# Ranking token scores: comparisons summed on VectorE, and comparisons summed by TensorE products with a column of ones

## The chip, the cores and the metric

The kernel runs on one core of one Trainium2 chip. The metric is the time on the device in microseconds (us). Three runs of the kernel before took 2085.96, 2092.15 and 2094.51 us; the median is 2092.15 us.

## The reference, cut to what matters

The model embeds 4 sequences of 1024 tokens (192 numbers each) and sends them through two layers. The change touches one step of the first layer's feed-forward block: a router scores every token, and the 154 tokens with the lowest scores (15% of 1024) get attention.

```
scores = jax.nn.sigmoid(jnp.einsum('bld,d->bl', normed, Wr) + br)
k = max(1, int(round(ROUTE_FRAC * l)))
_, idx = jax.lax.top_k(-scores, k)
attn_mask = jnp.zeros((b, l), bool).at[jnp.arange(b)[:, None], idx].set(True)
...
merged = jnp.where(attn_mask[..., None], attn_out, mix_out)
```

The order among the selected tokens has no meaning, but every one of them needs a slot of its own. The kernel gives each token its rank, the number of tokens of its sequence that come before it: those with a lower score, and of those with the same score the ones at an earlier position.

## The kernel before, in words

The four sequences are worked on as two pairs (`p` = 0, 1), one after the other. The two sequences of a pair live in two slots, `a` (x = 0) and `z` (x = 1), and nearly every step of the program is written as "for both slots". Tokens lie on partitions in T = 8 blocks of P = 128; L is 1024. There is no scheduler: each engine has its program written out by hand, runs it strictly in that order, and waits on semaphores. `link` lets an engine wait for the end of its own last instruction.

Around the change the order is this, on each engine:

- TensorE: `scores_row` for slot a, then `scores_row` for slot z. Each turns the scores from partitions into a row that is copied on all 128 partitions (8 transposes, L591), and then sums the tokens weighted by score: 24 products with a column of scores, N = 1 (L596). Then `pick` for slot a and for slot z (L603): 16 products that gather the selected tokens. Then `queries0` for both slots (L536, L551).
- ScalarE: copies the row of scores to SBUF, `srow` (L1191), for a and z; later it copies out what `pick` gathered (L1195).
- VectorE: `rank_tokens` for slot a, `pool_tokens` for slot a, then the same two for slot z. `rank_tokens` holds the change.

`rank_tokens` before: for each block t of 128 tokens, whose scores `sc[:, t]` lie one on a partition, VectorE compares the whole row `srow` with the partition's score and sums the ones of each partition in the same instruction (`accum_out`). The tokens from block t on are compared with "lower" (L1366), those of earlier blocks with "lower or equal" (L1368), and a 128x128 piece settles equal scores inside the block with the mask `earlier` (L1369). The three counts are added (L1371, L1372). From the ranks come `notsel` (L1374) and the selection matrix `PSEL` (L1376), whose semaphore `picks` releases `pick` on TensorE.

In the trace an instruction of VectorE with a sum shows as two records, the work and a short DVE_READ_ACCUMULATOR. One product of f32 operands shows as two matmuls and two weight loads (LDWEIGHTS), and a bf16 product as one of each; such a load with its matmul is called a pass below. The names in the trace: `R` holds `srow`, `Er` is a large work area (junk of the comparisons and `PSEL`), `PV` and `MT` are the PSUM banks `o.O` of slots a and z, `ST` and `S` are other PSUM banks.

Of the kernel before, what the change touches and what calls it, by code (L numbers as in the profile page):

```python
# [12 lines left out]
P = 128  # L13
# [4 lines left out]
L = 1024  # L18
# [66 lines left out]
def build(nc, A, out):  # L85
    ctx = ExitStack()
    with ctx:
        def sb(name, shape, dt=F32):
            return ctx.enter_context(nc.sbuf_tensor(name, shape, dt))
# [7 lines left out]

        ident = sb("ident", [P, P])
        identb = sb("identb", [P, P], BF16)
        earlier = sb("earlier", [P, P])  # L100
        ones = sb("ones", [P, P])
        neghalf = sb("neghalf", [P, T])
        slot = sb("slot", [P, 2, QP])
# [51 lines left out]
        junkg = acc_out[:, :, :].rearrange("p a n -> p (a n)")[:, 0:F]  # L155
        acc_mem = sb("acc_mem", [P, HALF])
        junk2 = sb("junk2", [P, P])
        vsum = junk2[:, 0:4 * VC].rearrange("p (t d) -> p t d", t=4)
        nmp = sb("nmp", [P, T, 2])
        nm = sb("nm", [P, T, 2])  # L160
# [8 lines left out]
        for x in range(2):  # L169
            o = Slot()  # L170
            slots.append(o)
            o.x = x
            nx = str(x)
            o.s = {n: sem("s_" + n + nx) for n in OWN}
            o.X = sb("X" + nx, [P, T, D])
            o.U = sb("U" + nx, [P, T, D])
            o.HS = sb("HS" + nx, [P, T, D])
            o.V = sb("V" + nx, [P, T, H, VC])
            o.XT = sb("XT" + nx, [CH + 1, 2, L])
            R = sb("R" + nx, [P, 4 * (L + 2)])  # L180
            o.R = R
            o.XC = R[0:CH, 0:2 * (L + 2)].rearrange("p (c n) -> p c n", c=2)
            o.CUM = o.XC[:, :, 2:L + 2]
            o.Y1 = R[0:CH, 2052:2052 + L]
            o.Z = R[0:CH, 3076:3076 + L]
            o.spl = R[0:CH, 0:3 * L].bitcast(BF16).rearrange("p (a c n) -> p a c n", a=3, c=2)
            o.srow = R[:, 3 * L:4 * L]
            o.PT = R[:, 0:2 * L].rearrange("p (q n) -> p q n", q=2)
            o.hid = R[:, 0:FC * HALF].rearrange("p (f n) -> p f n", f=FC)
            o.kc = R[0:CH, 0:3 * HALF].bitcast(BF16).rearrange("p (a n) -> p a n", a=3)  # L190
            o.qc = R[0:CH, 3 * HALF:6 * HALF].bitcast(BF16).rearrange("p (a n) -> p a n", a=3)
            o.BT = R[0:CH, 0:2 * L].rearrange("p (c n) -> p c n", c=2)
            o.HG = R[:, 0:HT * F].rearrange("p (t f) -> p t f", t=HT)
            o.PSEL = Er[:, x * W0:(x + 1) * W0].rearrange("p (t n) -> p t n", t=T)
            low, mid = Er[:, x * 1792:x * 1792 + 768], Er[:, x * 1792 + 768:x * 1792 + 1792]
            o.XQ = low.bitcast(BF16).rearrange("p (t d) -> p t d", t=T)
            o.XQT = mid[0:CH, :].bitcast(BF16).rearrange("p (c n) -> p c n", c=2)
            o.e2 = mid[:, 0:768].rearrange("p (i t d) -> p i t d", i=2, t=2)
            o.HQ = low.bitcast(BF16)
            o.HQT = Er[:, 3584 + x * 768:3584 + (x + 1) * 768].bitcast(BF16).rearrange("p (t f) -> p t f", t=2)  # L200
            o.QS0 = sb("QS0" + nx, [KP + 4, H, 2 * QP], BF16)
            o.NTS = sb("NTS" + nx, [CH + 1, 2, 2 * QP])
            o.CXT = o.NTS
            small = sb("small" + nx, [CH, 6 * QP])
            o.spl0 = small[:, :].bitcast(BF16).rearrange("p (a c n) -> p a c n", a=3, c=2)
            o.CX = small[0:QP, 0:2 * D].rearrange("p (q d) -> p q d", q=2)
            o.ATS = sb("ATS" + nx, [QP, 2, D])
            flat = o.X[0:QP, 0:3, :].rearrange("p t d -> p (t d)")
            o.sum0 = flat[:, 0:24 * VC].rearrange("p (n d) -> p n d", d=VC)
            o.rec0 = o.X[0:QP, 3, 0:24]  # L210
            o.st = sb("st" + nx, [P, T, 6])
            o.mv = sb("mv" + nx, [P, T, 2])
            o.rn = sb("rn" + nx, [P, T])
            o.rnn = sb("rnn" + nx, [P, T])
            o.tp = sb("tp" + nx, [P, T])
            o.sc = sb("sc" + nx, [P, T])
            o.sc1 = sb("sc1" + nx, [P, T])
            o.cnt = sb("cnt" + nx, [P, 3, T])
            o.rank = sb("rank" + nx, [P, T])
            o.notsel = sb("notsel" + nx, [P, T])  # L220
            o.pool3 = sb("pool3" + nx, [CH, 8])
            o.amax = sb("amax" + nx, [P, T])
            o.qsc = sb("qsc" + nx, [P, T])
            o.qinv = sb("qinv" + nx, [P, T])
            o.gsc = sb("gsc" + nx, [P, T])
            o.gsc2 = sb("gsc2" + nx, [P, T])
            o.ss = sb("ss" + nx, [P, T])

            o.ST = ST[x]
            o.R2 = [ring4[2 * x], ring4[2 * x + 1]]  # L230
            o.S = S[x][:, :]
            o.O = [PV[:, :], MTf][x]
            o.D2 = [o.O, o.S]
            o.scr_k0 = nc.dram_tensor("scr_k0" + nx, (3, D, L), BF16, kind="Internal").ap()
            o.scr_k = nc.dram_tensor("scr_k" + nx, (3, D, L), BF16, kind="Internal").ap()
            o.scr_q = nc.dram_tensor("scr_q" + nx, (3, D, L), BF16, kind="Internal").ap()
            o.scr_q0 = nc.dram_tensor("scr_q0" + nx, (3, D, 2 * QP), BF16, kind="Internal").ap()
# [10 lines left out]
        w1 = slots[0].X[:, 0:FC, :]  # L248
        w2 = slots[0].R[0:CH, 0:2 * F].rearrange("p (t f) -> p t f", t=2)

        names = """loaded consts tokens outproj h1 logit expz score srow_turned srow_copied picks rank_turned pt gathersel nts
            units0 reduced0 units reduced rowmax mturned mcopied acc0 ctxr accout st0 ex0 pv0 ctxn ctxt ctxtc att atts
            pooled mixin mixed merged stile exps pv alpha alphae fusedx fproj h3 quant qturned qcopied
            vlink plink filled pp pa pd kr0 kr1 kr2 kr3 qr0 qr1 qr2 qr3 q0w q0r mw mr""".split()
# [135 lines left out]
                sp.wait_ge(o.s["stored"], NPAIR * 32 + 32)  # L390

        LOADED = loads[0] * 16
        NCONST = 14

        @block.gpsimd
        def _(g):
            k = [0]

            def link(ins):

                k[0] += 1
                ins.then_inc(s["plink"], 1)
                g.wait_ge(s["plink"], k[0])
# [10 lines left out]
            link(g.memset(ident[:], 0.0))  # L414
            link(g.affine_select(out=ident[:], in_=ident[:], compare_op=ALU.not_equal, fill=1.0, base=0, pattern=[[-1, P]], channel_multiplier=1))
            const(g.tensor_copy(identb[:], ident[:]))
            link(g.memset(earlier[:], 1.0))
            const(g.affine_select(out=earlier[:], in_=earlier[:], compare_op=ALU.is_gt, fill=0.0, base=0, pattern=[[-1, P]], channel_multiplier=1))
            const(g.memset(ones[:], 1.0))
            const(g.memset(neghalf[:], -0.5))  # L420
            link(g.iota(slot_i, pattern=[[QC, 2], [1, QP]], base=0, channel_multiplier=0))
# [8 lines left out]
            for o in slots:  # L430
                const(g.memset(o.NTS[CH:CH + 1, :, :], 1.0))
                link(g.memset(o.QS0[KP:KP + 4, :, :], 0.0))
                const(g.memset(o.cnt[:], 0.0))

            def rsqrt(o, dst, src, eps, h=slice(0, T)):
                link(g.tensor_scalar(o.tp[:, h], src, eps, None, ALU.add))  # L436
# [40 lines left out]
        def _(pe):  # L477
# [109 lines left out]
            def scores_row(p, o):  # L587
                pe.wait_ge(s["score"], at(p, o, 1, 1))
                pe.wait_ge(o.s["resid"], p * 14 + 4)
                for t in range(T):  # L590
                    ins = nc.tensor.transpose(o.ST[:, t * P:(t + 1) * P], o.sc[:, t:t + 1].to_broadcast([P, P]), ident[:])  # L591
                ins.then_inc(s["srow_turned"], 1)
                for j in range(3):
                    for t in range(T):
                        lhs = o.X[:, t, j * CH:(j + 1) * CH] if j < 2 else ones[:, 0:CH]
                        ins = nc.tensor.matmul(o.O[0:CH, 16 + j:17 + j], lhs, o.sc[:, t:t + 1], start=t == 0, stop=t == T - 1)  # L596
                ins.then_inc(s["pooled"], 1)

            def pick(p, o):
                pe.wait_ge(s["picks"], at(p, o, 2, 2))  # L600
# [359 lines left out]
            for p in range(NPAIR):  # L960
# [11 lines left out]
                for o in slots:  # L972
                    scores_row(p, o)
                for o in slots:
                    pick(p, o)
                for o in slots:
                    queries0(p, o)
# [274 lines left out]
        def _(ve):  # L1252
# [109 lines left out]

            def rank_tokens(p, o):
                ve.wait_ge(s["srow_copied"], at(p, o, 1, 1))
                for t in range(T):
                    v.tensor_scalar(junkr[:, 0:L - t * P], o.srow[:, t * P:L], o.sc[:, t:t + 1], 0.0, ALU.is_lt, ALU.add, accum_out=o.cnt[:, 0, t:t + 1])  # L1366
                    if t > 0:
                        v.tensor_scalar(junkr[:, L - t * P:L], o.srow[:, 0:t * P], o.sc[:, t:t + 1], 0.0, ALU.is_le, ALU.add, accum_out=o.cnt[:, 1, t:t + 1])  # L1368
                    link(v.scalar_tensor_tensor(out=junk2[:], in0=o.srow[:, t * P:(t + 1) * P], scalar=o.sc[:, t:t + 1], in1=earlier[:], op0=ALU.is_equal, op1=ALU.mult,  # L1369
                                                accum_out=o.cnt[:, 2, t:t + 1]))  # L1370
                link(v.tensor_tensor(o.rank[:], o.cnt[:, 0, :], o.cnt[:, 1, :], ALU.add))  # L1371
                v.tensor_tensor(o.rank[:], o.rank[:], o.cnt[:, 2, :], ALU.add).then_inc(s["picks"], 1)  # L1372
                ve.wait_ge(s["picks"], at(p, o, 2, 1))
                v.tensor_scalar(o.notsel[:], o.rank[:], float(NSEL), None, ALU.is_ge)  # L1374
                for t in range(T):
# [293 lines left out]
```

## Time and profile before

| | |
|---|---|
| median of three runs | 2092.15 us (2085.96 to 2094.51) |
| the profiled execution's own time | 2091.71 us |
| its span, first to last instruction | 2089.9 us |
| TensorE, matmuls | 1704.3 us busy, 82% |
| VectorE | 1434.7 us busy, 69% |
| ScalarE | 961.2 us busy, 46% |
| GpSimd | 120.0 us busy, 6% |

The span is the time of the hardware profiler from the first to the last instruction; 1.8 us of the execution lie around it. Busy shares are means over stages that have different limits, so that what a step is worth has to be read at its place: which engine works there and which waits. In the page the engines are PE (TensorE), PEld (its weight loads), DVE (VectorE), ACT (ScalarE), POOL (GpSimd) and SP (SyncE). The clock granted to TensorE (PEclk) has two levels, 0.50 (1.2 GHz) and 1.00 (2.4 GHz); a value between them is the mean of a stretch with both.

### The profile page before, as it was taken

How to read it: one execution, taken by the hardware profiler on the slowest of the kernel's cores; microseconds unless marked ns; L12 is line 12 of the kernel's file. 1: busy time of each engine (PE TensorE's matmuls, PEld its weight loads, DVE VectorE, ACT ScalarE, POOL GpSimd, SP SyncE). 2: the span in 40 equal slices, each digit the busy share in tenths (PEclk: the TensorE clock that was granted, in tenths of full speed). 3: DMA queues.
4: the chain of work that ended last, by engine and by line, in shares of the span. 5: the costliest groups of instructions: out<-in, count | busy, mean ns of one | idle time of the engine just before them, and what ended most of it. 6: DMA issues, size and time to landing. Idle time of an engine off the chain costs nothing.

```text
span 2089.9 us, 27559 instructions
## 1 busy us (share of the span) xinstructions
PE 1704.3 (82%) x9834; PEld 957.4 (46%) x9834; DVE 1434.7 (69%) x3304; ACT 961.2 (46%) x1371; POOL 120.0 (6%) x163
## 2 busy tenths in 40 slices
PE   1686878898999999974466968789989999999445
PEld 1265547665333434363244654575633433335423
DVE  3757685215889898767768578740469898984876
ACT  0421341214677777831531324312347777776153
POOL 5010000000000000005011000000000000000100
PEclk9966897899899999996568678969989999999756
DMA  6001220002211010001000212000131010100000
GB/s 139 0 6 56 48 50 1 0 1 72 64 25 31 24 31 24 9 1 29 2 31 0 61 25 55 20 0 0 34 87 32 24 31 24 31 16 1 0 1 30
DMA packets 57644, 58.48 MB, mean 28 GB/s; under 512 B 27063, under 2 KB 35556, under 8 KB 57510
## 3 DMA queue, kind: packets, MB, share of 16 engines
q1 hardware_dynamic: 55894, 53.57, 10.1%
q0 software_dynamic: 1616, 3.16, 0.7%
q8 instruction: 79, 1.29, 0.3%
q14 instruction: 55, 0.45, 0.1%
HBM read 38.51 MB, written 18.16 MB: 27 GB/s over the span
## 4 chain that ended last, share of the span: by engine, by line
PE 64%; DVE 28%; ACT 3%; issue 3%; SPq 1%; DMA 1%; POOL 0%; DVEq 0%; ACTq 0%
PE PV L841 9%; PE ST L825 8%; PE S L791 6%; PE ST L737 4%; DVE nmp L1423 4%; PE ST L536 4%; PE MT L791 3%; PE PV L850 2%; DVE Er L1509 2%; PE PV L656 2%; DVE st L1311 2%; PE S L748 2%; DVE R L1529 1%; DVE amax L1530 1%; PE ST L563 1%
## 5 line engine op out<-in xcount | busy, mean ns | idle before, releaser
L1146 ACT ACTIVATE Er<-ST 128x1024 f32<-128x1024 f32 x384 | 377.1, 1021 | 105.7 <-PE ST L825 105.4
L1485 DVE TENSOR_REDUCE nmp<-S 128x1 f32<-128x512 f32 x514 | 337.6, 683 | 30.7 <-PE S L791 30.7
L825 PE MATMUL ST<-QS,KS 100*128 100x512 bf16 x768 | 218.0, 385 | 0.3
L841 PE MATMUL PV<-Er,V 128*17 128x512 f32 x1536 | 211.7, 600 | 0.0
L791 PE MATMUL S<-KS,QS 96*128 96x512 bf16 x514 | 183.3, 392 | 0.8
L1485 DVE TENSOR_REDUCE nmp<-MT 128x1 f32<-128x512 f32 x254 | 173.5, 683 | 13.5 <-PE MT L791 13.5
L1423 DVE TENSOR_REDUCE nmp<-S 80x1 f32<-80x512 f32 x192 | 120.1, 679 | 25.9 <-PE S L626 24.4
L791 PEld LDWEIGHTS S<-KS,QS 96*128 96x128 bf16 x514 | 48.3, 98 | 154.8 <-DVE nmp L1485 105.6
L436 POOL TENSOR_SCALAR tp<-mv 128x8 f32<-128x8 f32 x20 | 5.2, 259 | 1800.2 <-DVE mv L1315 1800.2
L626 PE MATMUL S<-KS,QS 96*80 96x512 bf16 x192 | 80.0, 448 | 34.1 <-DVE nmp L1423 31.4
L1113 ACT ACTIVATE Er<-ST 128x480 f32<-128x480 f32 x144 | 65.3, 527 | 83.5 <-PE ST L643 83.5
L825 PEld LDWEIGHTS ST<-QS,KS 100*128 100x128 bf16 x768 | 72.1, 99 | 64.3 <-ACT Er L1146 5.7
L791 PE MATMUL MT<-KS,QS 96*128 96x512 bf16 x254 | 99.4, 391 | 0.8 <-DVE nmp L1485 0.8
L737 PE MATMUL ST<-XT,wf 96*128 96x512 f32 x192 | 84.0, 593 | 0.0
L949 PE MATMUL S<-identb,Er 128*128 128x128 bf16 x192 | 23.7, 293 | 70.2 <-DVE Er L1545 70.2
L1340 DVE TENSOR_TENSOR acc_out<-ST,R 96x512 f32<-96x512 f32 x48 | 32.9, 685 | 67.6 <-ACT R L1068 56.4
L1058 ACT ACTIVATE XT<-PV,cols 96x512 f32<-96x512 f32 x8 | 6.2, 774 | 154.9 <-PE PV L518 154.9
L1164 ACT ACTIVATE R<-ST 128x512 f32<-128x512 f32 x48 | 28.7, 598 | 93.4 <-PE ST L737 93.4
L1453 DVE TENSOR_TENSOR HS<-PV,HS 128x384 f32<-128x384 f32 x8 | 4.5, 558 | 92.2 <-PE PV L749 82.5
L1148 ACT ACTIVATE Er<-ST 100x1024 f32<-100x1024 f32 x48 | 49.2, 1025 | 28.3 <-PE ST L829 28.3
L1246 ACT ACTIVATE Er<-S 128x768 bf16<-128x768 bf16 x32 | 25.5, 810 | 77.3 <-PE S L949 77.3
L841 PEld LDWEIGHTS PV<-Er,V 128*17 128x17 f32 x1536 | 32.4, 95 | 62.2 <-issue 60.5
(382 smaller groups left out, 3337.4 us busy)
## 6 DMA issues: line engine op xcount, KB each, us to landing
KS<-scr_k SPq DMA_DIRECT2D x576, 32.0 KB, 1.8
scr_k<-R SPq DMA_DIRECT2D x16, 576.0 KB, 3.9
QS<-scr_q SPq DMA_DIRECT2D x288, 32.0 KB, 1.8
scr_q<-R SPq DMA_DIRECT2D x8, 576.0 KB, 3.7
out_dram<-HS SPq DMA_DIRECT2D x8, 384.0 KB, 2.8
QS<-scr_q SPq DMA_DIRECT2D x48, 30.0 KB, 1.9
wf<-in_L_ffn_W_dram SPq DMA_DIRECT2D x2, 576.0 KB
scr_q<-small SPq DMA_DIRECT2D x8, 90.0 KB, 2.0
```

Of the source, the lines that this page charges most:

```text
L536: ins = nc.tensor.matmul(o.R2[i % 2][0:CH, 0:width], w[0:r, c, off + m * CH:off + (m + 1) * CH], src[0:r, c, j * width:(j + 1) * width], s ...
L626: nc.tensor.matmul(S[n % 2][0:QP, :], o.QS0[0:KP, h % H, (u // 2) * QP:(u // 2 + 1) * QP], KS[0:KP, h % KRING, (u % 2) * HALF:(u % 2 + 1) ...
L656: ins = nc.tensor.matmul(PV[row:row + VC, (j % 3) * 2 * QP:(j % 3 + 1) * 2 * QP], o.V[:, kt, h % H, :], E0[:, h % RING0, kt * 2 * QP:(kt + ...
L737: ins = nc.tensor.matmul(o.R2[i % 2], wf1[0:r, c, f * P:(f + 1) * P], o.XT[0:r, c, half * HALF:(half + 1) * HALF], start=c == 0, stop=c == 1)
L791: ins = nc.tensor.matmul(bank, QS[0:KP, k, (u // 2) * P:(u // 2 + 1) * P], KS[0:KP, k, (u % 2) * HALF:(u % 2 + 1) * HALF], start=True, sto ...
L825: ins = nc.tensor.matmul(ST[i % 2][:, (kt % 2) * HALF:(kt % 2 + 1) * HALF], KS[0:KP + 4, k, kt * P:(kt + 1) * P], QS[0:KP + 4, k, half * H ...
L841: ins = nc.tensor.matmul(PV[row:row + VC, :], slots[h // H].V[:, kt, h % H, :], E[:, step % RING, (kt % 2) * HALF:(kt % 2 + 1) * HALF], st ...
L1113: A_(E0[:, h % RING0, i * 6 * QP:i * 6 * QP + w], ring4[n % 4][:, 0:w], ACT.Exp, scale=float(DH) ** -0.5).then_inc(s["ex0"], 1)
L1146: A_(E[:, g, :], ST[i % 2][:, :], ACT.Exp).then_inc(s["exps"], 1)
L1148: A_(E[0:MS, g, :], ST[i % 2][0:MS, :], ACT.Exp).then_inc(s["exps"], 1)
L1423: v.tensor_reduce(nmp[0:QP, u // 2, u % 2:u % 2 + 1], S[n % 2][0:QP, :], AX.X, ALU.max).then_inc(s["reduced0"], 1)
L1485: v.tensor_reduce(nmp[:, u // 2, u % 2:u % 2 + 1], bank, AX.X, ALU.max).then_inc(s["reduced"], 1)
```

## The change

VectorE no longer sums. For each block `jt` of 128 tokens (now the tokens that are counted, one on a partition) it writes the comparisons with the whole row as bf16 ones and zeros into `below`, a ring of two rows of 1024, and those inside the block, by the mask `later`, into `same`, a ring of two pieces of 128. TensorE then counts: each 128x128 piece of ones and zeros is loaded as weights and multiplied by a column of ones (N = 1), so that the sums over the partitions land on the partitions of the tokens ranked. All 8 blocks add into one group of sums, `o.O[:, 32:40]`, which a product with zeros opens and another closes. VectorE copies the ranks from PSUM. TensorE's `count` stands ahead of `pick` in each slot. The buffer `cnt` and its two memsets on GpSimd are gone.

```diff
-        junkr = Er[:, 2 * W0:2 * W0 + L]
+        below = Er[:, 2 * W0:2 * W0 + L].bitcast(BF16).rearrange("p (r n) -> p r n", r=2)
...
+        same = junk2[:, :].bitcast(BF16).rearrange("p (r n) -> p r n", r=2)
+        zerob = ones[:, 0:T].bitcast(BF16).rearrange("p (t b) -> p t b", b=2)[:, :, 0]
+        oneb = ones[:, 0:1].bitcast(BF16)[:, 1:2]
...
-                const(g.memset(o.cnt[:], 0.0))
...
+            def count(p, o):
+
+                nc.tensor.matmul(o.O[:, 32:32 + T], identb[:], zerob, start=True, stop=False)
+                for jt in range(T):
+                    pe.wait_ge(s["compared"], at(p, o, T, jt + 1))
+                    for it in range(T):
+                        ins = nc.tensor.matmul(o.O[:, 32 + it:33 + it], below[:, jt % 2, it * P:(it + 1) * P], oneb, start=False, stop=False)
+                    ins = nc.tensor.matmul(o.O[:, 32 + jt:33 + jt], same[:, jt % 2, :], oneb, start=False, stop=False)
+                    if jt == T - 1:
+                        ins = nc.tensor.matmul(o.O[:, 32:32 + T], identb[:], zerob, start=False, stop=True)
+                    ins.then_inc(s["counted"], 1)
...
                 for o in slots:
+                    count(p, o)
                     pick(p, o)
...
             def rank_tokens(p, o):
                 ve.wait_ge(s["srow_copied"], at(p, o, 1, 1))
-                for t in range(T):
-                    v.tensor_scalar(junkr[:, 0:L - t * P], o.srow[:, t * P:L], o.sc[:, t:t + 1], 0.0, ALU.is_lt, ALU.add, accum_out=o.cnt[:, 0, t:t + 1])
-                    if t > 0:
-                        v.tensor_scalar(junkr[:, L - t * P:L], o.srow[:, 0:t * P], o.sc[:, t:t + 1], 0.0, ALU.is_le, ALU.add, accum_out=o.cnt[:, 1, t:t + 1])
-                    link(v.scalar_tensor_tensor(out=junk2[:], in0=o.srow[:, t * P:(t + 1) * P], scalar=o.sc[:, t:t + 1], in1=earlier[:], op0=ALU.is_equal, op1=ALU.mult,
-                                                accum_out=o.cnt[:, 2, t:t + 1]))
-                link(v.tensor_tensor(o.rank[:], o.cnt[:, 0, :], o.cnt[:, 1, :], ALU.add))
-                v.tensor_tensor(o.rank[:], o.rank[:], o.cnt[:, 2, :], ALU.add).then_inc(s["picks"], 1)
+                for jt in range(T):
+                    if p or o is z or jt >= 2:
+                        ve.wait_ge(s["counted"], at(p, o, T, jt - 1))
+                    c, n = below[:, jt % 2, :], (jt + 1) * P
+                    v.tensor_scalar(c[:, 0:n], o.srow[:, 0:n], o.sc[:, jt:jt + 1], None, ALU.is_gt)
+                    if jt < T - 1:
+                        v.tensor_scalar(c[:, n:L], o.srow[:, n:L], o.sc[:, jt:jt + 1], None, ALU.is_ge)
+                    v.scalar_tensor_tensor(out=same[:, jt % 2, :], in0=o.srow[:, jt * P:n], scalar=o.sc[:, jt:jt + 1], in1=later[:],
+                                           op0=ALU.is_equal, op1=ALU.mult).then_inc(s["compared"], 1)
+                ve.wait_ge(s["counted"], at(p, o, T, T))
+                v.tensor_copy(o.rank[:], o.O[:, 32:32 + T]).then_inc(s["picks"], 1)
```

The order on TensorE, in the first pair, from `scores_row` of slot a to `pick` of slot a. Before:

```order
L596 MATMUL PV<-sc,ones 96x1 x8
L591 MATMUL ST<-ident,sc 128x128 [waits s_resid1,s_score]
L591 MATMUL ST<-ident,sc 128x128 x7
L596 MATMUL MT<-sc,X 96x1 x16
L596 MATMUL MT<-sc,ones 96x1 x8
L603 MATMUL S<-Er,X 96x160 [waits s_picks]
L603 MATMUL S<-Er,X 96x160 x15
L603 MATMUL S<-Er,X 96x160 [waits s_picks]
```

With the change, from the same place on (`Er` is now also `below`, `junk` is `same`, `ones` the column of ones or the zeros):

```order
L592 MATMUL ST<-ident,sc 128x128 [waits s_resid1,s_score]
L592 MATMUL ST<-ident,sc 128x128 x7
L597 MATMUL MT<-sc,X 96x1 x16
L597 MATMUL MT<-sc,ones 96x1 x8
L602 MATMUL PV<-ones,identb 128x8
L606 MATMUL PV<-ones,Er 128x1 [waits s_compared]
L606 MATMUL PV<-ones,Er 128x1 x7
L607 MATMUL PV<-ones,junk 128x1
L606 MATMUL PV<-ones,Er 128x1 [waits s_compared]
L606 MATMUL PV<-ones,Er 128x1 x7
L607 MATMUL PV<-ones,junk 128x1
L606 MATMUL PV<-ones,Er 128x1 [waits s_compared]
```

The first counting product for slot a stands behind all 24 products of `scores_row` for slot z. Eight such groups of nine stand ahead of `pick` for slot a, and eight more between the two picks.

The order on VectorE at the start of `rank_tokens` for slot a. Before:

```order
L1366 TENSOR_SCALAR Er,cnt<-R,sc 128x1024 [waits s_srow_copied]
L1369 SCALAR_TENSOR_TENSOR junk,cnt<-R,sc,earlier 128x128
L1366 TENSOR_SCALAR Er,cnt<-R,sc 128x896 [waits s_vlink]
L1368 TENSOR_SCALAR Er,cnt<-R,sc 128x128
L1369 SCALAR_TENSOR_TENSOR junk,cnt<-R,sc,earlier 128x128
L1366 TENSOR_SCALAR Er,cnt<-R,sc 128x768 [waits s_vlink]
```

And with the change:

```order
L1383 TENSOR_SCALAR Er<-R,sc 128x128 [waits s_srow_copied]
L1385 TENSOR_SCALAR Er<-R,sc 128x896
L1386 SCALAR_TENSOR_TENSOR junk<-R,sc,later 128x128
L1383 TENSOR_SCALAR Er<-R,sc 128x256
L1385 TENSOR_SCALAR Er<-R,sc 128x768
L1386 SCALAR_TENSOR_TENSOR junk<-R,sc,later 128x128
L1383 TENSOR_SCALAR Er<-R,sc 128x384 [waits s_counted]
L1385 TENSOR_SCALAR Er<-R,sc 128x640
L1386 SCALAR_TENSOR_TENSOR junk<-R,sc,later 128x128
L1383 TENSOR_SCALAR Er<-R,sc 128x512 [waits s_counted]
```

The instructions are as many and as wide. The waits of VectorE for itself are gone, and from the third block on each block waits for TensorE's count of the block two before it.

## Rows read from the trace of the kernel before

**Rows 1.** The page: busy time, and shares of the chain that ended last.
```profile
PE 1704.3 (82%) x9834; PEld 957.4 (46%) x9834; DVE 1434.7 (69%) x3304; ACT 961.2 (46%) x1371; POOL 120.0 (6%) x163
PE 64%; DVE 28%; ACT 3%; issue 3%; SPq 1%; DMA 1%; POOL 0%; DVEq 0%; ACTq 0%
```
**Rows 2.** Timeline, first pair: start, us, engine, line, tiles, count, idle before.
```profile
171.32 1.28 DVE L1366 TENSOR_SCALAR_CACHE_REDUCE Er<-R,sc 128x1024 f32<-128x1024 f32 x1 [0.22 <-ACT R L1191]
...
174.00 4.80 PE L596 MATMUL MT<-sc,X 128*96 128x1 f32 x32
...
178.67 2.70 PE L596 MATMUL MT<-sc,ones 128*96 128x1 f32 x16
...
185.22 0.17 DVE L1372 TENSOR_TENSOR rank<-rank,cnt 128x8 f32<-128x8 f32 x1
...
185.50 1.78 DVE L1376 TENSOR_SCALAR Er<-slot,rank 128x160 f32<-128x160 f32 x8
...
187.33 6.60 PE L603 MATMUL S<-Er,X 128*96 128x160 f32 x32 [5.97 <-DVE Er L1376]
...
202.42 0.17 DVE L1372 TENSOR_TENSOR rank<-rank,cnt 128x8 f32<-128x8 f32 x1
...
204.54 6.53 PE L603 MATMUL S<-Er,X 128*96 128x160 f32 x32 [10.61 <-DVE Er L1376]
```
**Rows 3.** The chain of waits, first pair: start, us, what.
```profile
202.79 1.71 DVE Er L1376 x8
204.54 6.53 PE S L603 x32
211.07 1.09 PE ST L536 x8
```
**Rows 4.** VectorE by line: duration in ns, least/median/most, and forms.
```profile
L1358 DVE TENSOR_SCALAR R<-R,cols x8: 748/749/751, 85.3 to 1128.8; 96x1024 f32<-96x1024 f32 x8
L1376 DVE TENSOR_SCALAR Er<-slot,rank x32: 295/296/297, 185.5 to 1221.4; 128x160 f32<-128x160 f32 x32
L1369 DVE SCALAR_TENSOR_TENSOR junk<-R,sc,earlier x32: 346/348/349, 172.5 to 1219.0; 128x128 f32<-128x128 f32 x32
L1304 DVE TENSOR_SCALAR Er<-X x1: 761/761/761, 46.3 to 46.3; 128x1152 bf16<-128x1152 f32 x1
```
**Rows 5.** Timeline, bf16 weight loads and matmuls, at 1011.7 and 253.0 us.
```profile
1011.71 0.56 PEld L949 LDWEIGHTS S<-identb,Er 128*128 128x128 bf16 x6 [10.44 <-DVE Er L1545]
1011.71 0.82 PE L949 MATMUL S<-identb,Er 128*128 128x128 bf16 x6 [9.96 <-DVE Er L1545]
253.02 0.53 PEld L643 LDWEIGHTS ST<-QS,KS 98*128 98x128 bf16 x8 [0.47 <-issue]
```
**Rows 6.** f32 products with N = 1: by line (ns), and in the chain of waits.
```profile
L596 PE MATMUL PV<-sc,X x64: 167/223/223, 169.1 to 1188.8; 128*96 128x1 f32 x64
L596 PE MATMUL MT<-sc,X x64: 167/298/300, 174.0 to 1195.7; 128*96 128x1 f32 x64
139.94 4.69 PE PV L583 x22
```
**Rows 7.** Windows: stretch, us, busy and count of PE, PEld, DVE, ACT, POOL; PEclk; DMA.
```profile
1011.70:1012.60 0.90, 0.82 (x6) 0.56 (x6) 0.87 (x2) 0.03 (x1) 0.00 (x0) 0.50 0.00 0
253.00:253.80 0.80, 0.80 (x13) 0.69 (x10) 0.00 (x0) 0.36 (x1) 0.00 (x0) 1.00 0.00 0
176.00:181.40 5.40, 5.36 (x34) 5.28 (x33) 5.29 (x21) 0.00 (x0) 0.00 (x0) 0.50 0.03 12
187.30:190.80 3.50, 3.47 (x13) 3.47 (x14) 3.25 (x11) 0.00 (x0) 0.00 (x0) 0.50 0.02 5
204.50:208.00 3.50, 3.46 (x13) 3.46 (x14) 1.02 (x6) 0.00 (x0) 0.00 (x0) 0.50 0.00 0
```
**Rows 8.** Timeline, the second pair's picks.
```profile
1204.53 6.59 PE L603 MATMUL S<-Er,X 128*96 128x160 f32 x32 [5.95 <-DVE Er L1376]
1221.74 6.52 PE L603 MATMUL S<-Er,X 128*96 128x160 f32 x32 [10.62 <-DVE Er L1376]
```
**Rows 9.** Timeline: the end of slot z's pick; GpSimd's last memset and first gather.
```profile
209.82 1.25 PE L603 MATMUL S<-Er,X 128*96 128x160 f32 x8
13.33 0.12 POOL L433 MEMSET cnt<- 128x24 f32 x1
14.17 1.10 POOL L455 DMA_INDIRECT U<-_L_tok_embed_matrix_dram,tok_i  x1 [0.71 <-POOL cnt L433]
```
**Rows 10.** The chain of waits in the prologue.
```profile
19.32 14.47 DMA R<-in_L_ffn_w_dram
```

More of the change, by code:

```diff
@@ L99, in build @@
         identb = sb("identb", [P, P], BF16)
-        earlier = sb("earlier", [P, P])
+        later = sb("later", [P, P])
         ones = sb("ones", [P, P])
@@ L217, in build @@
             o.sc1 = sb("sc1" + nx, [P, T])
-            o.cnt = sb("cnt" + nx, [P, 3, T])
             o.rank = sb("rank" + nx, [P, T])
@@ L249, in build @@
         w2 = slots[0].R[0:CH, 0:2 * F].rearrange("p (t f) -> p t f", t=2)
-        names = """loaded consts tokens outproj h1 logit expz score srow_turned srow_copied picks rank_turned pt gathersel nts
+        names = """compared counted loaded consts tokens outproj h1 logit expz score srow_turned srow_copied picks rank_turned pt gathersel nts
             units0 reduced0 units reduced rowmax mturned mcopied acc0 ctxr accout st0 ex0 pv0 ctxn ctxt ctxtc att atts
@@ L392, in build @@
         LOADED = loads[0] * 16
-        NCONST = 14
+        NCONST = 12
         @block.gpsimd
@@ L416, in _ @@
             const(g.tensor_copy(identb[:], ident[:]))
-            link(g.memset(earlier[:], 1.0))
-            const(g.affine_select(out=earlier[:], in_=earlier[:], compare_op=ALU.is_gt, fill=0.0, base=0, pattern=[[-1, P]], channel_multiplier=1))
+            link(g.memset(later[:], 1.0))
+            const(g.affine_select(out=later[:], in_=later[:], compare_op=ALU.is_gt, fill=0.0, base=0, pattern=[[1, P]], channel_multiplier=-1))
             const(g.memset(ones[:], 1.0))
```

## The prediction

> **What bounds the kernel now.** I read the page first. Its chain of work that ended last is 64% TensorE and 28% VectorE, though VectorE is busy 69% of the span [rows 1]: these means don't say who is waited for in the ranking, so I went to the timeline of that stretch, to the chain of waits there, and last to the rows by line for the price of each operation.
>
> In the timeline [rows 2] VectorE begins to rank slot a at 171.32 us. Its last addition starts at 185.22, the selection matrix is written from 185.50, and `pick` of slot a starts at 187.33, after TensorE has been idle for 5.97 us. VectorE goes on to slot z without a gap, adds up at 202.42, and `pick` of slot z starts at 204.54, after 10.61 us of idle TensorE. The chain of waits runs through the matrix of slot z, its pick and the query projection behind it [rows 3]. So what ends the ranking is paid one for one, twice per pair of sequences; the second pair shows the same picks [rows 8].
>
> The same rows show what the change will meet. TensorE is not free when VectorE starts: it works on the score sums of slot z (L596) from 174.00 until 178.67 + 2.70 = 181.37, hidden behind VectorE. In the order of the changed kernel these sums stand ahead of the first count.
>
> **The change part by part.** VectorE. Before, the ranking takes 185.22 - 171.32 = 13.90 us for eight blocks, 1.7 a block. A comparison without a sum, from SBUF to SBUF, with a column as scalar takes 749 ns for 1024 numbers and 295 for 160 [rows 4]: 0.525 ns a number and 0.21 us fixed. The bf16 output costs nothing, since 1152 numbers to bf16 take 761 ns. Back to back, eight of 295 ns take 1.78 us [rows 2], so each starts (1.78 - 0.295)/7 = 0.212 after the last and 0.083 is overlapped. A block has two comparisons of together 1024 numbers, 0.54 + 2 x 0.13 = 0.80, and the piece with equal scores, 0.347 - 0.083 = 0.26 [rows 4]: it costs VectorE 1.06 us, and 1.14 from its first start to its end. If nothing held it up, eight blocks would take 8.5 us, 5 less than before.
>
> But it is held up. The ring has two rows, so block 2 waits for the count of block 0, and that can't start before 181.37. VectorE is through with blocks 0 and 1 at about 173.5 and then stands for 9 us. What is queued behind it there is nothing that could fill the time: its own pooling and slot z come later in its order.
>
> A count on TensorE. A block is nine bf16 passes with N = 1, which the trace does not have. The nearest rows are bf16 loads of the same 128x128 shape [rows 5]: six in 0.56 us, the last one 0.147 long, which is 0.083 a load, at a granted clock of 0.50 [rows 7]; and eight in 0.53, 0.062 a load, at 1.00. Passes with N = 1 and f32 operands (two per product) with 128 columns take 4.69/22 = 0.213 [rows 6], with 96 columns 4.80/32 = 0.150 [rows 2], both at 0.50. From below the bound is almost nothing, as the loads could be held back by their wide matmuls. I take 0.083 and 0.062, since these rows have the type and the shape. The last pass adds the length of a matmul with N = 1, 0.30 or 0.22 [rows 6]. A group thus takes 8 x 0.083 + 0.30 = 0.96 us at the low clock and 0.72 at the high one, and I add 0.05 for each signal between engines: the matrix ends at 187.28 and TensorE starts at 187.33 [rows 2].
>
> Slot a. The clock is at 0.50 when the sums of slot z end [rows 7]. The opening pass and block 0 take 9 x 0.083 + 0.30 = 1.05, so VectorE starts block 2 at 181.37 + 1.05 + 0.05 = 182.47. From here a block of VectorE (1.14) and its count with both signals (1.06) are passed back and forth over two rows, 1.10 a block. Block 7 ends at 182.47 + 5 x 1.10 + 1.14 = 189.11; its count and the closing pass take 0.05 + 1.05 + 0.05, and the ranks are copied at 190.26. That copy stands where the addition at 185.22 stood: 5.04 us later. The rest up to `pick` is unchanged, so it runs from 192.37 to 198.97.
>
> Slot z. VectorE finishes the matrix and the pooling of slot a and writes its blocks 0 and 1 during that pick, but TensorE turns to the counts only at 198.97. The clock has risen in the pick, so block 0 is counted after 9 x 0.062 + 0.22 = 0.78, and VectorE starts block 2 at 199.80. Now VectorE is the slower one, 5 x 1.06 + 1.14 = 6.4: it ends at 206.2. The clock may have fallen again by then; with 1.05 + 0.1 for the last count the copy is at 207.4, against 202.42: 5.0 us later, and this is what the chain sees.
>
> The sum. 5.0 us a pair, two pairs, +10.0 us. The two memsets of `cnt` on GpSimd (0.12 us each [rows 9]) go for nothing: the gathers behind them would start a little earlier, but the prologue waits for a weight transfer that takes until 33.8 us [rows 10]. All that follows `pick` of slot z hangs on it, so I let nothing absorb the shift. The profiled execution took 2091.71 us, 0.4 below the median of the runs shown; 2091.7 + 10.0 = 2101.7 us, 0.46% above that median.
>
> **What the Trainium skill says to it.** The rows gave 0.083 us a load at the low clock and 0.062 at the high one. The Trainium skill, in "TensorE: Matmul & The Clock Gate", section "LDWEIGHTS (loading the stationary operand)", makes a load cost its columns divided by 1.2, in ns, which is 0.107 us for 128 columns. The trace is below that at both clocks. By that rule the sum would be the lower price of the first rival below, whose own working follows from rows.
>
> **The rivals.** First, the passes are slower than these loads, and TensorE becomes the bound of the loop (the other side: slower by more than can be mistaken). A pass with N = 1 has no wide matmul behind which the next load hides, and the f32 passes speak for it. At half the f32 pass with 128 columns, 0.107, at either clock, a group takes 1.16 and a block 1.20. Slot a: 181.37 + 1.26 + 0.05 + 6.00 + 1.14 + 1.36 = 191.2, 6.0 late; slot z begins at 199.9 and ends by the same terms at 209.7, 7.3 late; +14.6, 2106.3 us. At 0.150 (and 0.088 where the clock is high) slot a ends at 192.9 and slot z at 211.6, 9.2 late; +18.4, 2110.1. It decides from about 0.08 a pass, where the group with its signals outlasts VectorE's block. At the full 0.213 it would be some 2126; I leave that outside.
>
> Second, the clock (not slower by anything that can be told). Today TensorE idles before each pick, and the first 3.5 us of a pick are granted 0.50 [rows 7]; its passes take 0.27 us there (13 in 3.5) and 1.25/8 = 0.156 at its end [rows 9]. If the counts keep the clock up, a pick takes 32 x 0.156 = 5.0 and not 6.6. Both picks of a pair are in the new chain, so 5.0 - 3.2 = 1.8 a pair remain: +3.6, 2095.3 us. Against it: in the sums of slot z TensorE was busy 5.36 of 5.40 us with products of N = 1, and was granted 0.50 all the while [rows 7]; the counts are the same kind of work, less dense. The table "Why this matters for your kernels" of "TensorE: Matmul & The Clock Gate" in the Trainium skill says to keep TensorE busy to get the full clock; the trace has a busy TensorE without it.
>
> Third, comparisons with a column and a bf16 output run at one number per cycle, as the sums do (1.28 us for 1024 [rows 2]), not at the rate of 749 ns. That adds 0.53 to each of the six late blocks of a slot, 3.2 a slot and 6.4 a pair, less a little slack: about 2114 us. No row has column and bf16 output in one instruction, though each alone is fast.
>
> **How the numbers follow.** About 0.5% (10.5 us) is what a measurement of this kernel can tell from no change, and my sum sits just inside it. Chances: the forecast, 2097 to 2105 us, 0.62, of which 0.37 is within 0.5% and 0.25 over it; slow passes 0.16; the clock 0.14, of which 0.12 within and 0.02 faster; slow comparisons 0.04; something in the later stages that moves with the shift, either way, 0.04 (0.03 faster). Together faster 0.05, same 0.49, slower 0.46. The range is 2095 to 2111 us: from the clock's case to the upper price of slow passes.
>
> **What would show it.** In the changed profile: a stand of about 9 us on VectorE before the third block of slot a, ended by the count, in both pairs, and one of about 3 us before that of slot z; comparisons of together 1.06 us a block; 1.06 to 1.10 us from block to block; nine passes in 0.7 to 1.0 us; `pick` of slot a near 192.4 and of slot z near 209.5, with 0.50 at its start. Passes of 0.11 and more would show the first rival, picks of 5 us the second. I am wrong at the root if VectorE does not stand there, or if the stages behind slot z's pick do not shift with it.

## The result, and the profile after

The changed kernel takes 2100.01 us (median of 15 runs, 2094.88 to 2104.28), the kernel before on the same chip 2091.38 us (15 runs, 2085.96 to 2094.51). The ratio is 1.0038, with a 95% interval of 1.0029 to 1.0047: 7.9 us more, 6.1 to 9.8. The forecast was 2101.7 us. The profiled execution took 2100.6 us with a span of 2098.8, against 2091.71 and 2089.9.

The page of the changed kernel, busy time and the shares of the chain that ended last, to be read against [rows 1]:

```profile
PE 1725.7 (82%) x10130; PEld 973.5 (46%) x10130; DVE 1414.0 (67%) x3208; ACT 961.6 (46%) x1371; POOL 119.5 (6%) x161
PE 66%; DVE 26%; ACT 3%; issue 2%; SPq 1%; DMA 1%; POOL 0%; DVEq 0%; ACTq 0%
```

VectorE has 20.7 us less work and TensorE 21.4 more. The chain moved with them, and the time did not fall. The timeline of the first pair says why (start, us, engine, line, tiles, shape, count, and in brackets the idle time before it with what ended it):

```profile
170.12 0.29 DVE L1383 TENSOR_SCALAR Er<-R,sc 128x128 bf16<-128x128 f32 x1 [0.22 <-ACT R L1205]
...
172.80 4.79 PE L597 MATMUL MT<-sc,X 128*96 128x1 f32 x32
...
177.46 2.70 PE L597 MATMUL MT<-sc,ones 128*96 128x1 f32 x16
...
180.02 0.29 PEld L606 LDWEIGHTS PV<-ones,Er 128*128 128x128 bf16 x8
...
180.23 0.10 PEld L607 LDWEIGHTS PV<-ones,junk 128*128 128x128 bf16 x1
...
180.46 0.42 DVE L1383 TENSOR_SCALAR Er<-R,sc 128x384 bf16<-128x384 f32 x1 [8.15 <-PE PV L607]
...
181.52 0.48 DVE L1383 TENSOR_SCALAR Er<-R,sc 128x512 bf16<-128x512 f32 x1
...
182.57 0.55 DVE L1383 TENSOR_SCALAR Er<-R,sc 128x640 bf16<-128x640 f32 x1
...
182.72 0.37 PE L606 MATMUL PV<-ones,Er 128*128 128x1 bf16 x8 [0.65 <-DVE junk L1386]
...
182.95 0.17 PE L607 MATMUL PV<-ones,junk 128*128 128x1 bf16 x1
...
187.27 0.17 DVE L1389 COPY rank<-PV 128x8 f32<-128x8 f32 x1 [0.52 <-PE PV L609]
...
189.39 6.68 PE L616 MATMUL S<-Er,X 128*96 128x160 f32 x32 [2.15 <-DVE Er L1393]
...
195.91 0.27 PEld L606 LDWEIGHTS MT<-ones,Er 128*128 128x128 bf16 x8
...
196.11 0.10 PEld L607 LDWEIGHTS MT<-ones,junk 128*128 128x128 bf16 x1
...
196.34 0.42 DVE L1383 TENSOR_SCALAR Er<-R,sc 128x384 bf16<-128x384 f32 x1 [3.57 <-PE MT L607]
...
203.14 0.17 DVE L1389 COPY rank<-MT 128x8 f32<-128x8 f32 x1 [0.52 <-PE MT L609]
...
205.26 7.27 PE L616 MATMUL S<-Er,X 128*96 128x160 f32 x32 [2.16 <-DVE Er L1393]
```

This execution's ranking starts 1.20 us earlier than before's, so I measure from VectorE's first comparison. The copy of slot a's ranks comes 17.15 us after it; the addition that it replaces came 13.90 us after [rows 2]: 3.25 later. Slot z's copy comes at 33.02 against 31.10: 1.92 later. Its `pick` ends at 42.41 against 39.75: 2.66 later, since the pick itself takes 7.27 us and not 6.53. The second pair gives 42.41 and 39.75 again. The ranking therefore costs 5.3 us. Between the kernels the time differs by 7.9 (6.1 to 9.8), so 1 to 4.5 us arise elsewhere. The later stages do move with the pick: from its end to the second pair's first comparison it is 978.2 us here (212.53 to 1190.71) and 977.4 before. VectorE stands 8.15 us in slot a, and the second pair shows the same:

```profile
1201.08 0.42 DVE L1383 TENSOR_SCALAR Er<-R,sc 128x384 bf16<-128x384 f32 x1 [8.17 <-PE PV L607]
```

The chain of waits of the changed kernel in this stretch now has TensorE's sums, the first count and the last count in it:

```profile
172.96 7.19 PE MT L597 x48
...
180.19 0.21 PE PV L606 x8
...
180.46 0.42 DVE Er L1383
...
186.80 0.37 PE PV L606 x8
...
187.27 0.18 DVE rank L1389
...
189.39 6.68 PE S L616 x32
```

And the windows of the changed kernel for the sums and the two picks' beginnings (stretch, us, busy of PE, PEld, DVE, ACT, POOL, PEclk, DMA share, GB/s):

```profile
173.50:181.20 7.70, 7.16 (x61) 7.08 (x61) 0.74 (x2) 0.52 (x1) 0.00 (x0) 0.50 0.11 38
187.00:192.00 5.00, 2.85 (x19) 2.76 (x17) 4.49 (x21) 0.00 (x0) 0.00 (x0) 0.50 0.00 0
196.00:199.00 3.00, 1.28 (x38) 1.01 (x36) 2.67 (x8) 0.86 (x2) 0.00 (x0) 1.00 0.00 0
203.00:207.00 4.00, 1.84 (x11) 1.76 (x9) 3.06 (x16) 0.00 (x0) 0.00 (x0) 0.50 0.00 0
207.00:210.00 3.00, 3.00 (x13) 3.00 (x12) 0.00 (x0) 0.00 (x0) 0.00 (x0) 0.50 0.00 0
```

The granted clock is 0.50 in the sums, 1.00 in the first counts of slot z, and 0.50 from the last counts into its pick.

### The profile page after: what moved, and what is told of

It is laid out like the page before. It is cut to its first block, busy times and chain, and to the rows that moved or that the text cites. A ratio compares the mean times of both kernels' runs of the same rounds, so it can differ in the third digit from the quotient of the medians.

```text
span 2098.8 us, 28054 instructions
## 1 busy us (share of the span) xinstructions
PE 1725.7 (82%) x10130; PEld 973.5 (46%) x10130; DVE 1414.0 (67%) x3208; ACT 961.6 (46%) x1371; POOL 119.5 (6%) x161
## 4 chain that ended last, share of the span: by engine, by line
PE 66%; DVE 26%; ACT 3%; issue 2%; SPq 1%; DMA 1%; POOL 0%; DVEq 0%; ACTq 0%
PE PV L854 9%; PE ST L838 8%; PE S L804 6%; PE ST L750 4%; DVE nmp L1440 4%; PE ST L537 4%; PE MT L804 3%; PE PV L863 2%; DVE Er L1526 2%; PE PV L669 2%; DVE st L1325 2%; PE S L761 2%; PE S L639 1%; DVE R L1546 1%; DVE amax L1547 1%
```

## The experiments

Ratios are to the kernel before, run beside it on the same chip. "Shift" is taken from each trace: the time from VectorE's first comparison to the end of slot z's pick, less before's 39.75 us, both pairs added. It holds what the pick itself gained or lost in length.

| kernel | median us (runs) | ratio (95%) | shift us |
|---|---|---|---|
| changed kernel, again | 2096.82 (8) | 1.0032 (1.0017 to 1.0046) | +5.3 |
| every pass twice | 2100.33 (5) | 1.0059 (1.0044 to 1.0073) | +6.0 |
| sums woven in | 2085.66 (12) | 0.9992 (0.998 to 1.0004) | -8.1 |
| ring of five | 2086.5 (12) | 0.9992 (0.9978 to 1.0006) | -8.0 |
| both | 2077.36 (6) | 0.9943 (0.9925 to 0.9961) | -15.1 |
| before, 1.2 us of delay | 2086.12 (11) | 0.9992 (0.9979 to 1.0006) | +1.2 |
| before, 2.66 us of delay | 2097.59 (6) | 1.0046 (1.0028 to 1.0064) | +5.6 |
| before, 5.0 us of delay | 2104.54 (5) | 1.0079 (1.0065 to 1.0093) | +11.8 |

**Slot z's sums woven into the counts.** The order alone: two of slot z's sums stand behind each count of slot a, the last eight ahead of its pick.

```diff
+            def pool_sums(p, o, n0=0, n1=3 * T):
...
                     ins.then_inc(s["counted"], 1)
+                    if o is a:
+                        pool_sums(p, z, 2 * jt, 2 * jt + 2)
...
-                for o in slots:
-                    scores_row(p, o)
-                for o in slots:
-                    count(p, o)
-                    pick(p, o)
+                scores_row(p, a)
+                pool_sums(p, a)
+                scores_row(p, z)
+                count(p, a)
+                pool_sums(p, z, 2 * T)
+                pick(p, a)
+                count(p, z)
+                pick(p, z)
```

> The changed kernel (2100.0 us), with one thing moved: the 24 score sums of slot z no longer stand ahead of the first count. Two of them follow each of the eight counts of slot a, and the last eight stand between the counts and the pick of slot a. Theory (the queue): the counts begin at about 173.0 us instead of 179.9, VectorE's stand of 8.15 us before the third block of slot a shrinks to about 1, and its rank copy moves from 187.3 to about 180.4; slot z stays as it is relative to the pick of slot a, so a pair gains 6.5 to 7 us: 2086 to 2088 us, below the kernel before (2091.4). Rival (the handshake): passing each block between the engines is what costs, wherever the counts start; then the copy comes at 185 or later and the time stays above 2097 us. Rival (crowding): the sums between the counts hold the counts up, so that the loop takes over 1.2 us a block: about 2090 us.

The timeline of this kernel, first pair:

```profile
170.29 0.42 DVE L1391 TENSOR_SCALAR Er<-R,sc 128x384 bf16<-128x384 f32 x1 [0.92 <-PE PV L610]
...
177.10 0.17 DVE L1397 COPY rank<-PV 128x8 f32<-128x8 f32 x1 [0.52 <-PE PV L612]
...
186.80 0.42 DVE L1391 TENSOR_SCALAR Er<-R,sc 128x384 bf16<-128x384 f32 x1 [4.20 <-PE MT L610]
...
195.72 7.14 PE L621 MATMUL S<-Er,X 128*96 128x160 f32 x32 [2.15 <-DVE Er L1401]
```

The stand of 8.15 us is 0.92 here, and the ranks of slot a are copied 9.93 us after the start instead of 17.15. No instruction was added or taken away, so the stand was queue order. In slot z, where the pick of slot a is in the way, 4.20 us stay. The expectation foretold this stretch rightly, but also a time 3 to 5 us below the kernel before. Against before, run beside it, the time is unchanged (-1.7 us, interval -4.2 to +0.8), though the shift is -8.1 us: a second question, taken up below.

**A ring of five rows.** TensorE's order stays; VectorE may run five blocks ahead instead of two.

```diff
-        below = Er[:, 2 * W0:2 * W0 + L].bitcast(BF16).rearrange("p (r n) -> p r n", r=2)
+        below = Er[:, 2 * W0:2 * W0 + 5 * L // 2].bitcast(BF16).rearrange("p (r n) -> p r n", r=5)
-        same = junk2[:, :].bitcast(BF16).rearrange("p (r n) -> p r n", r=2)
+        same = sb("same", [P, 5, P], BF16)
...
-                    if p or o is z or jt >= 2:
-                        ve.wait_ge(s["counted"], at(p, o, T, jt - 1))
-                    c, n = below[:, jt % 2, :], (jt + 1) * P
+                    g = at(p, o, T, jt)
+                    if g >= 5:
+                        ve.wait_ge(s["counted"], g - 4)
+                    c, n = below[:, g % 5, :], (jt + 1) * P
```

> The changed kernel (2100.0 us) with five rows of comparisons in the ring instead of two; TensorE's order is as it was. Theory (the ring): VectorE writes blocks 0 to 4 while TensorE is at the sums of slot z, and again while it is at the pick of slot a; three blocks less are behind the wait in each slot. Rank copy of slot a 3.1 us earlier (184.2), pick of slot z 6 us earlier in each pair: about 2088 us. If the loss lay in the handshake, a deeper ring would gain only the slack between 1.06 and the loop's period, which the profile shows to be nothing: 2099 to 2100 us.

Its timeline, the sixth block of each slot:

```profile
175.76 0.62 DVE L1385 TENSOR_SCALAR Er<-R,sc 128x768 bf16<-128x768 f32 x1 [5.03 <-PE PV L608]
...
188.31 0.62 DVE L1385 TENSOR_SCALAR Er<-R,sc 128x768 bf16<-128x768 f32 x1 [0.24 <-PE MT L608]
```

Three rows more save three blocks of waiting in each slot: 8.15 - 5.03 = 3.12 and 3.57 - 0.24 = 3.33 us, which is 3 x 1.05. The stands were where the forecast put them, and the ring's depth sets what VectorE can do in them. Against before the time is again unchanged (-1.7 us, -4.6 to +1.3), with a shift of -8.0.

**Both together.**

> Both of the other edits: score sums of slot z woven behind the counts of slot a, and a ring of five rows. By both theories: slot a is then bound by VectorE alone (eight blocks of 1.06 and 0.5 for the last count, copy at about 179.3), slot z has three blocks behind the pick of slot a. Pick of slot z about 10.5 us earlier than in the changed kernel in each pair: 2079 us, 12 below the kernel before. If the two edits removed the same wait, the gain would be that of the better one alone, about 2087 us.

Its timeline, first pair:

```profile
180.53 0.17 DVE L1399 COPY rank<-PV 128x8 f32<-128x8 f32 x1 [0.77 <-PE PV L613]
...
183.55 6.80 PE L622 MATMUL S<-Er,X 128*96 128x160 f32 x32
...
190.62 0.62 DVE L1393 TENSOR_SCALAR Er<-R,sc 128x768 bf16<-128x768 f32 x1 [1.42 <-PE MT L611]
...
196.37 7.23 PE L622 MATMUL S<-Er,X 128*96 128x160 f32 x32 [2.16 <-DVE Er L1403]
```

VectorE doesn't stand in slot a, and 1.42 us in slot z; slot z's pick ends 7.5 us earlier than before's. This version beats both kernels; by its ratio it is 11.9 us faster than the kernel before (8.1 to 15.7).

**Every counting pass twice.** Each block is counted twice, and the copy halves the ranks.

```diff
-                    for it in range(T):
+                    for it in (*range(T), *range(T)):
...
-                v.tensor_copy(o.rank[:], o.O[:, 32:32 + T]).then_inc(s["picks"], 1)
+                v.tensor_scalar(o.rank[:], o.O[:, 32:32 + T], 0.5, None, ALU.mult).then_inc(s["picks"], 1)
```

> The changed kernel with every counting pass done twice (the ranks are halved when they are copied, so they stay the same). Nine passes took 0.23 us from first load to last load, so a block's count grows by as much. Theory (VectorE is the slower one in the loop, and only the first and the last count of a slot are waited for): 0.25 to 0.5 a slot, 1 to 2 us in all over the changed kernel, and the loop keeps 1.05 us a block. Rival (TensorE's passes bound the loop): 0.23 for each of eight blocks, 7 us or more in all.

Its timeline: 16 passes of `Er`, then two starts of VectorE's blocks two blocks apart, and the passes of a later group:

```profile
180.07 0.50 PEld L606 LDWEIGHTS PV<-ones,Er 128*128 128x128 bf16 x16
...
180.75 0.42 DVE L1384 TENSOR_SCALAR Er<-R,sc 128x384 bf16<-128x384 f32 x1 [8.51 <-PE PV L608]
...
182.86 0.55 DVE L1384 TENSOR_SCALAR Er<-R,sc 128x640 bf16<-128x640 f32 x1
...
183.00 0.59 PE L606 MATMUL PV<-ones,Er 128*128 128x1 bf16 x16 [0.41 <-DVE junk L1387]
```

Sixteen loads take 0.50 us where eight took 0.29: 8 more for 0.21, 0.026 a pass. VectorE's blocks still follow each other by 1.05 us ((182.86 - 180.75) / 2), so TensorE is not the bound of the loop even with twice the passes: it still waits 0.41 us for each block. The shift of both pairs is 0.7 us over the changed kernel's. By ratios it costs 0.27% more, 5.6 us, and by medians 3.5: more than the 1 to 2 that I expected of it. Of that the ranking in its trace shows only the 0.7; where the rest arises these traces don't show.

**A delay in the kernel before.** Does the change cost anything beside its shift? Useless work on VectorE, 2.66 us long, stands ahead of slot z's selection matrix; nothing else is changed. Two more sizes, 1.2 and 5.0 us, use other widths.

```diff
                 ve.wait_ge(s["picks"], at(p, o, 2, 1))
+                if o is z:
+                    for u, w in ((0, L), (L, L), (2 * L, P)):
+                        v.scalar_tensor_tensor(out=Er[:, 2 * W0 + u:2 * W0 + u + w], in0=o.srow[:, 0:w], scalar=o.sc[:, 0:1], in1=o.srow[:, 0:w], op0=ALU.mult, op1=ALU.add)
                 v.tensor_scalar(o.notsel[:], o.rank[:], float(NSEL), None, ALU.is_ge)
```

> The kernel before (2091.4 us) with 2.66 us of VectorE work that nobody needs (two comparisons-like operations of 1.2 us and one of 0.26) put ahead of the selection matrix of slot z in each pair. It prices a pure shift. In the profiles of the two kernels the selected rows of slot z are ready 2.66 us later per pair than before, 5.3 us in all, but the time grew by 8.6 (medians). Theory (the rest is the clock): a pure shift of 2.66 us costs 5.3 us, up to 1 more or less by where the clock changes fall, 2096 to 2098 us; then what lies beyond is either scatter of the clock or due to TensorE's counts. Rival (a shift costs more than itself): some stage behind the pick amplifies it, and the time is 2099 to 2101 us, as with the change.

It came to +9.6 us instead of +5.3, as much as the change itself costs. So a kernel without a single count, but late by the same amount at the same place, is as slow: no further cost of the counts is needed. But the shift does not look paid one for one, although the interval (5.8 to 13.4) almost reaches the 5.6 of its trace. The other sizes and the changed kernel once more were to show by what rule it is paid:

> The kernel before with one needless operation of 1.2 us of VectorE ahead of the selection matrix of slot z in each pair: a pure shift of 2.4 us in all. Before it, a shift of 2.66 a pair (5.3 us in all) was measured as 9.6 (5.8 to 13.4). Theory (a shift costs itself, and the rest is where the clock changes): +2 to +4 us. Rival (something behind the pick doubles a shift): +5 us.

> The same with four needless operations and two waits for itself, 5.0 us ahead of the matrix of slot z in each pair: a shift of 10.0 us in all. Theory (a shift costs itself): +8 to +12 us, so that the surplus of the middle dose does not grow with the dose. Rival (doubling): +17 to +20 us.

> The changed kernel itself, run again beside the next ones on one chip, to compare them with it. Ratio to the kernel before 1.003 to 1.005, some 6 to 10 us.

The short delay costs nothing (-1.7 us, interval -4.4 to +1.3), so its expectation of +2 to +4 failed; the long one costs 16.5 (13.6 to 19.4), where I had expected 8 to 12 and named 17 to 20 as the rival's. The changed kernel repeats, with +6.7. Part of this is in slot z's pick itself, which follows the delay. First the short one, then the long one, in their first pairs:

```profile
198.85 5.95 PE L603 MATMUL S<-Er,X 128*96 128x160 f32 x32 [11.80 <-DVE Er L1379]
...
205.48 7.40 PE L603 MATMUL S<-Er,X 128*96 128x160 f32 x32 [15.65 <-DVE Er L1381]
```

They start 1.20 and 5.03 us later than before's, measured from the first comparison (34.42 and 38.25 against 33.22), but take 5.95 and 7.40 us instead of 6.53. That is why the shifts are +1.2 and +11.8 and not the 2.4 and 10.0 that the delays alone would make.

**What goes with the rest: TensorE's mean clock.** Each run has its mean granted clock. The eighteen runs of the kernel before beside the last four kernels go from 2085.46 us at 0.868 to 2093.95 at 0.860: one program, no shift at all, 8 us. A line through all runs of one chip, with one slope and a level of its own for each kernel, gives 0.96 us (0.79 to 1.13) for each 0.001 of clock on the one chip, and 1.15 us (0.99 to 1.31) on the other. The levels are the kernels' times at equal clock, less before's; all bounds are 95%:

| kernel | shift | at equal clock | by medians | mean clock less before's |
|---|---|---|---|---|
| changed kernel, again | +5.3 | +5.0 ± 1.3 | +7.7 | -0.0016 |
| every pass twice | +6.0 | +6.7 ± 1.7 | +11.2 | -0.0047 |
| sums woven in | -8.1 | -8.5 ± 1.4 | -1.1 | -0.0060 |
| ring of five | -8.0 | -7.9 ± 1.3 | -0.3 | -0.0056 |
| both | -15.1 | -14.0 ± 1.4 | -9.4 | -0.0037 |
| 1.2 us of delay | +1.2 | -0.7 ± 1.2 | -3.0 | +0.0016 |
| 2.66 us of delay | +5.6 | +3.3 ± 1.6 | +10.8 | -0.0065 |
| 5.0 us of delay | +11.8 | +8.0 ± 2.0 | +15.4 | -0.0077 |

The kernels' mean clocks differ. All but the one with the short delay lie lower than before's, the woven order and the ring of five by 0.006; with the clock taken out these two show the gain of about 8 us that their times don't show. But the correction is crude, since the mean also holds the clock inside the ranking. There it is 0.66 over 39.8 us before, 0.64 over 42.4 us with the change, 0.63 over 45.7 with the long delay and 0.68 over 32.2 with both edits, in either pair. That alone moves the mean of the whole run by about -0.0017 (2 x (0.36 x 42.4 - 0.34 x 39.8) / 2090), -0.003 and +0.003. It is all of the difference that "changed kernel, again" has, and with that part left in, its level is +6.6 and not +5.0, the long delay's about +11 and that of both edits about -18. So the column is good to 3 or 4 us and not to its bounds of 1.2 to 2.0: within that, every kernel stands where its shift puts it, and nothing finer is shown.

Does the shift move the clock of the later stages? The traces give only a hint. Here is the stage behind slot z's pick, cut in stretches of 10 us from the pick's end. First the kernel before (columns as above, PEclk is the third from the right):

```profile
221.10:231.10 10.00, 6.46 (x27) 3.62 (x27) 6.77 (x13) 1.79 (x5) 0.00 (x0) 0.90 0.34 65
231.10:241.10 10.00, 9.61 (x42) 4.79 (x40) 8.74 (x21) 4.97 (x12) 0.00 (x0) 0.50 0.19 46
241.10:251.10 10.00, 9.03 (x70) 4.23 (x73) 6.91 (x17) 3.32 (x8) 0.00 (x0) 0.67 0.20 48
```

The changed kernel:

```profile
222.50:232.50 10.00, 6.78 (x27) 3.54 (x26) 6.69 (x12) 1.85 (x5) 0.00 (x0) 0.77 0.34 66
232.50:242.50 10.00, 9.61 (x43) 4.88 (x42) 8.67 (x21) 4.84 (x12) 0.00 (x0) 0.50 0.18 44
242.50:252.50 10.00, 9.74 (x62) 4.57 (x62) 6.59 (x15) 3.46 (x9) 0.00 (x0) 0.50 0.18 44
```

The kernel before with 1.2 us of delay:

```profile
214.80:224.80 10.00, 6.58 (x27) 3.65 (x27) 6.77 (x13) 1.82 (x5) 0.00 (x0) 0.87 0.32 65
224.80:234.80 10.00, 9.60 (x42) 4.80 (x40) 8.74 (x21) 4.97 (x12) 0.00 (x0) 0.50 0.19 44
234.80:244.80 10.00, 8.67 (x82) 4.54 (x85) 7.17 (x17) 3.31 (x8) 0.00 (x0) 0.78 0.19 49
```

All three fall to 0.50 behind the same thin stretch, in which TensorE is busy 6.5 to 6.8 of 10 us. They differ in when it falls and when it comes back. Of these 30 us the clock is low for 2 + 10 + 6.6 = 18.6 us in the kernel before (0.90 means a fifth of the stretch at 0.50), 24.6 in the changed one and 17.0 with the short delay. The whole stage takes 117.4 us before, 118.2 changed and 115.8 with the short delay; in the second pair it is 116.1, 118.1 and 115.8, and the stages behind it 745.5, 747.6 and 745.2. But one trace does not stand for its kernel. The second trace of the changed kernel has this for the stage in the first pair, in the second, and for all that is behind:

```profile
215.50:333.70 118.20, 97.08 (x837) 57.46 (x835) 84.33 (x217) 49.07 (x119) 0.00 (x0) 0.84 0.19 44
1236.10:1353.00 116.90, 95.66 (x837) 56.38 (x835) 84.34 (x217) 49.07 (x119) 0.00 (x0) 0.85 0.19 45
1353.00:2098.50 745.50, 641.10 (x3596) 341.31 (x3596) 516.43 (x1135) 389.81 (x502) 25.62 (x34) 0.89 0.08 22
```

The last two are 1.2 and 2.1 us shorter than in the first trace, with the same shift, and the last is as long as before's. In the woven order's trace the three take 117.7, 117.7 and 747.8 us, 4.2 more than in the one trace of before; this fits its lost gain, but differences of 3 us arise within one kernel too. What decides where the clock falls and comes back I can't say from these runs; no experiment changed it alone.

## Why the prediction was right, and which step was off

The time lay 1.7 us from the forecast, in the likeliest case's own range. The mechanism was right: VectorE stands behind TensorE's sums, and the picks come later by it. The closeness of the number is partly luck: one term was too large and one was left out. The change was to add 10.0 us and added 7.9, of which the ranking has 5.3.

- **The stand in slot a.** Foretold about 9 us, ended by the count, in both pairs: 8.15 and 8.17. The woven order shows that it comes from the sums ahead in the queue, the ring of five that the two rows turn it into a stand. In slot z about 3 us were foretold and 3.57 are there.
- **VectorE's block.** 1.06 us foretold, 1.05 measured (180.46 to 181.52), also with every pass doubled. The third rival is refuted: with a column and a bf16 output 384 numbers take 0.42 us.
- **The price of a pass, the mis-sized term.** I took the spacing of loads that had wide matmuls beside them [rows 5] as the price, 0.083 and 0.062 us. With N = 1 the load behind eight others starts 0.21 us after the first at a granted clock of 0.50 (180.02 to 180.23) and 0.20 at 1.00 (195.91 to 196.11), so a pass is 0.026 or 0.025 us, and the low clock doesn't double it. The lower bound "almost nothing" was nearer than the value I chose. Its reason, that the loads of those rows are held back by their matmuls, fits this, but no run varied the width of the matmuls. A block's count then is 0.4 us (182.72 to 183.12) and not 1.0. It stopped pacing the loop and both ends of each slot: slot a came 3.25 us late instead of 5.04 (0.8 of the difference before its third block, 0.35 in the loop, 0.6 at the last count), slot z 1.92 instead of 5.0. The rule of the Trainium skill, page "TensorE: Matmul & The Clock Gate", section "LDWEIGHTS (loading the stationary operand)", divides the columns by 1.2 to get a load's ns, an estimate of 0.107 us for 128. The recorded length of a load here is near it, 0.096 to 0.104 in most of them, but the spacing is a quarter of that: loads behind each other overlap. The first rival fell with it.
- **Nothing absorbs the shift: the term that was left out.** The later stages shifted with the pick, so nothing absorbed it. But the forecast put all that the change does elsewhere at nothing, and 2.6 us more were measured (0.8 to 4.5; in the second series 1.4, which its interval does not tell from nothing). The delays of 5.6 and 11.8 us were paid with 9.6 and 16.5, and that of 1.2 with nothing that can be told. "Something in the later stages" had a chance of 0.04, of which only 0.01 was for slower: too small. That it is the clock of those stages is argued from the mean clocks, not shown.
- **The clock in the picks.** The second rival hoped for picks of 5 us. They are 6.68 and 7.27 us, and their first microseconds are granted 0.50. Slot z's even got 0.74 us longer, which the forecast had at nothing too: 1.5 us of the ranking's 5.3.
- **The memsets and the prologue.** Nothing of them is visible: the start of the ranking differs by up to 9 us between the traces of these kernels (164.43 to 173.11), also where their prologues are the same. A single trace can be as much shorter or longer by its prologue alone.

By terms: 5.3 for the ranking instead of 10.0, and about 2.6 instead of 0 for the rest.

## What to carry to other kernels

When work moves from one in-order engine to another, look first at what already stands in the other's queue at the hour when the first piece arrives, and at how far the giver may run ahead. Here 7.2 us of hidden sums and a ring of two turned a saving of 0.65 us in each block into a loss, and another order with three more rows turned it into a gain of 0.6%. And where a kernel's runs spread with the granted clock, look at each kernel's mean clock beside its time: the woven order saves 8 us in the ranking, and its time shows none of it. Take more than one trace of a kernel before a difference of 3 us in a later stage is put down to the change.

## What the runs showed of the hardware

- A bf16 weight load of 128x128 with a matmul of N = 1 behind it costs 0.026 us in a row of such passes at a granted clock of 0.50 and 0.025 at 1.00. f32 passes of that kind took 0.150 us with 96 columns and 0.213 with 128 [rows 2, 6].
- From the end of the last comparison to the copy of the ranks lie 0.52 us, for the last block's count, the closing product and two signals; with twice the passes 0.76.
- The mean granted clock of one program varies between executions by 0.010 (0.860 to 0.870 in the 23 runs of the kernel before beside the first four kernels), and among runs of one kernel 0.001 less goes with about 1 us more of 2090 (0.96 and 1.15 on two chips).
- A pick of 32 f32 passes took 5.95 us when its start was 1.20 us later than before's, 6.53 before and 7.40 when it was 5.03 later: work that is only moved can change its length.
- Two executions of the changed kernel, with the same shift, differ by 3.3 us in the stages behind slot z's pick of the second pair.
- Slot z's sums kept TensorE busy 7.16 of 7.70 us with products of N = 1, and the clock stayed at 0.50; the first counts after slot a's pick ran at 1.00.
